# Level masks on VectorE two levels ahead, all row squares on GpSimd, four softplus parts among the third attention's last blocks

## The chip, the cores and the metric

The kernel runs on one core of one Trainium2 chip. Time is the device time of one execution in microseconds. Before the change it is 5413.46 us, the median of three runs (5405.54 to 5415.52).

## The reference, cut to what matters

Two decoder layers over x (64 x 128 x 256, float32) with a context of the same shape. Every residual block starts with a layer norm.

```
x += L0_attn(ln(x))    # gated delta rule, 2 heads of 128, chunks of 64
x += L0_xattn(ln(x))   # cross attention, 16 heads
x += L0_ffn(ln(x))     # 4 experts of width 512, top 2
x += L1_attn(ln(x))    # latent attention, causal
x += L1_xattn(ln(x))   # cross attention, causal
x += L1_ffn(ln(x))     # 8 experts of width 128, top 2
# in L0_attn, per chunk of 64 rows
log_decay = -exp(A_log) * softplus(x @ W_alpha.T + dt_bias)
cum = cumsum(log_decay);  L_mask = tril(exp(cum_i - cum_j))
M = tril(-(wk_scaled @ wk.T) * L_mask, -1)
A = inverse(eye - M)              # unit lower triangular
```

The first layer norm and the decays are computed with error-free sums and products (pairs of a value and its rounding rest), the rest in plain float32.

## The kernel before, in words

A loop of 16 passes takes four sequences each. Every engine has its own instruction list, written by hand and repeated with `Fori`; they meet only in semaphores, whose counts are written into the waits (`S[...]`, `sum_step`, `chain_step`, `au_ready`, `y_ready`). There is no planner: the order in the source is the order on each engine.

In one pass TensorE, ScalarE and VectorE carry the blocks in the order of the reference. The delta rule's inverse is built in six levels. `first_level` (L1635 on) makes MT, the level-0 matrix and `Um`. At level l, TensorE transposes `Um` (L1089) to `Tm`, multiplies it with a masked copy of MT, `lev[l % 2]` (L1067, counted in `W_psum`), multiplies the result with `Um` (L1074, `U_psum`), and VectorE adds that to `Um` (L1823). The read scores (L1046) and the values (L1054) go between levels on TensorE. The masked copies, MT times `levmask[l]`, are made by GpSimd at L647, two heads a level, twelve a pass.

GpSimd works ahead in the background on the decay projection of the next pass's rows. Its chain has four slices of 64 columns; each is 22 products (`chain_products`, 128x256 elements) and 16 links (`chain_links`, eight operations on 128x32). It is counted in `chain_step`. Slice 0's products lie between the level masks, in the shares of `LEVEL_PRODUCTS`. Between links GpSimd adds rows to the residual `xres`, after waits for the layer norm (`xn`), the root of the exact norm (`ref_step`), the mixture's statistics (`hl_mean`) and the router's gates (`g_w`); `ROUTER_LINKS` and the numbers in the calls say how many links lie between these. The chain ends with `au` (L678). Then `centered` sums and centres the rows of the pass after next (L503, the last step is a 128x1024 subtraction in `x_in`), and GpSimd waits for `y_ready`, makes the squares and adds rows 0 to 15 of 32 (`first_squares`), and builds the decay table (`decay_table`, which ends with `dec_beta`, needed by `first_level`). SP moves `x_in` to `xn_next` once `chain_step` has reached `CHAIN_READ`, and then loads the next x.

VectorE adds the other sixteen rows (`exact_squares(16, 32)`, L1425) in four pieces during the level stage, behind a wait for `sum_step`, and then takes the variance.

Softplus of `au` is a list of ten parts of three or four small operations on 128x10 elements (`decay_exponential`, tile `dec_t`), each behind a wait for its predecessor, followed by a quotient, a series, and `y_nat` (L1596). In the third attention VectorE runs 16 score blocks u (L1854 takes the maximum, L1858 subtracts it, both read PSUM) and, for each b of four, two operations on the outputs (L1875, L1877) that TensorE waits for at L1199. Parts 0 to 4, with the wait for `au`, lie ahead of the output operations of b = 2, parts 5 to 7 ahead of b = 3; parts 8 and 9 come after the last xT copy, ahead of the gates.

Of the kernel before, what the change touches and what calls it, by code (L numbers as in the profile page):

```python
# [12 lines left out]
ALU = mybir.AluOpType  # L13
# [6 lines left out]
P = 128  # L20
D = 256
C = D // P
G = 4
# [6 lines left out]
DH = 2  # L30
# [41 lines left out]
def decoder_kernel(nc, a, out):  # L72
# [7 lines left out]
    with ExitStack() as ctx:  # L80
# [362 lines left out]
        def _(pool):  # L443
# [79 lines left out]
            def first_squares(it, a):  # L523

                tt = pool.tensor_tensor
                w8 = sq.rearrange("p b (k n) -> p b k n", n=32)
                sum_link(it, a, tt, sq, x_in[:, :, :], x_in[:, :, :], ALU.mult)
                sum_link(it, a, tt, lan2[:, :, :], w8[:, :, :, 0], w8[:, :, :, 1], ALU.add)
                for k in range(2, 16):
                    sum_link(it, a, tt, lan2[:, :, :], lan2[:, :, :], w8[:, :, :, k], ALU.add)  # L530
                assert summed[0] == SUM_STEPS, summed[0]

# [92 lines left out]
            decay_table(0, 0)  # L625

            with nc.Fori(0, NIT, engines=[pool.engine], hint_back_edge=True) as it:
# [12 lines left out]
                for l in range(1, LEVELS):  # L640
                    chain_products(pool, link, src, 0, LEVEL_PRODUCTS[l - 1], LEVEL_PRODUCTS[l])
                    for h in range(DH):
                        if l == 1 and h == 0:
                            pool.wait_ge(S["inv_eye"], at(it, "inv_eye", 2))
                        if l > 2:
                            pool.wait_ge(S["W_psum"], at(it, "W_psum", 2 * (l - 3) + h + 1))
                        pool.tensor_tensor(heads(lev[:, l % 2, h, :]), heads(MT[:, h, :]),  # L647
                                           levmask[:, l, :].unsqueeze(1).broadcast_to([P, G, P]), ALU.mult).then_inc(S["lev"], 1)

# [4 lines left out]
                chain_links(pool, link, 0, 0, 5)  # L654
# [3 lines left out]
                chain_links(pool, link, 0, 5, 16)  # L658
# [12 lines left out]
                chain_links(pool, link, 3, 0, 8)  # L671
                pool.wait_ge(x_norm, nth(it, 1, 1, 2))
                assert linked[0] < CHAIN_READ, linked[0]
                chain_links(pool, link, 3, 8, 16)
# [7 lines left out]
                decay_table(it, 1)  # L682

# [682 lines left out]
        def _(dve):  # L1366
# [365 lines left out]
            with nc.Fori(0, NIT, engines=[dve.engine], hint_back_edge=True) as it:  # L1732
# [76 lines left out]
                xT_copy(0)  # L1809
                wait("ctx_psum", 2)  # L1810
                dve.tensor_copy(ctxT[:, 1, :], bank[3][:, :]).then_inc(S["ctxT_dve"], 1)
                dve.wait_ge(sum_step, nth(it, SUM_STEPS, SUM_STEPS))
                exact_squares(16, 21)
# [6 lines left out]
                for l in range(1, LEVELS - 1):  # L1820
                    for h in range(DH):
                        wait("U_psum", 2 * (l - 1) + h + 1)
                        dve.tensor_tensor(Um[:, h, :], Um[:, h, :], bank[4 + h][:, :], ALU.add).then_inc(S["U"], 1)  # L1823
                    if l == 1:
                        read_decays(0)
                        exact_squares(21, 25)
                    if l == 2:
                        read_decays(1)
                        exact_squares(25, 29)
                    if l == 3:  # L1830
                        exact_squares(29, 32)
                        exact_variance()
# [15 lines left out]
                def attention(a_no):  # L1848
                    base = a_no * QUADS
                    for u in range(QUADS + 8):  # L1850
                        if u < QUADS:
# [7 lines left out]
                            if a_no == 1 and u % 2:  # L1859
                                exact_rest(1, u // 4, u // 2 % 2)  # L1860
                        if u >= 6 and (u - 6) % 4 == 3 and (u - 6) // 4 < G:
# [5 lines left out]
                            if a_no == 2 and b == 2:  # L1867
                                for part in range(5):
                                    decay_exponential(part)
                            if a_no == 2 and b == 3:  # L1870
                                for part in range(5, 8):
# [193 lines left out]
                decay_exponential(8)  # L2065
# [33 lines left out]
ROUTER_LINKS = 5  # L2099
REF_STEPS = 75  # L2100
CHAIN_READ = 530
PRODUCTS = 22
LEVEL_PRODUCTS = (0, 4, 4, 8, 14, 19, 22)
ROOT_STEPS = 41
# [3 lines left out]
SUM_STEPS = 37  # L2108
# [30 lines left out]
```

## Time and profile before

| | |
|---|---|
| median of three runs | 5413.46 us |
| the profiled execution | 5405.82 us |
| its span, first to last instruction | 5403.9 us |
| TensorE busy | 4731.9 us (88%) |
| VectorE busy | 4303.5 us (80%) |
| GpSimd busy | 3938.4 us (73%) |
| ScalarE busy | 2323.7 us (43%) |
| mean granted TensorE clock | 0.954 |

The profile is of one execution. A line such as L1823 is a line of the kernel, PE is TensorE, DVE VectorE, ACT ScalarE, POOL GpSimd. PE has two sets of rows, its matmuls and its weight loads (PEld). Times in a timeline count from the first instruction. Most SBUF tiles are cuts of one tensor, `arena`, so many rows name only that.

### The profile page before, as it was taken

Reading aid. Unit: us, or ns where it says so; the run is one execution under the profiler, and the core shown is the slowest. Engines: PE = TensorE matmul, PEld = TensorE weight load, DVE = VectorE, ACT = ScalarE, POOL = GpSimd, SP = SyncE. Lnnn points to the kernel's source line nnn. Section 1 sums busy time; section 2 is a strip of 40 time slices with the busy share of each in tenths; the row PEclk is TensorE's granted clock in tenths of the full one; section 3 lists DMA queues with packets and bytes.
Section 4 is the critical chain, followed back from the end, with each engine's and each line's share of the span. In section 5 each row is a group of like instructions: output and inputs, shape, how many; then the busy total and the mean of one; then the engine's idle time right before and its main releaser. Section 6 shows DMA issues by size and latency. Waiting matters only on the chain.

```text
span 5403.9 us, 105986 instructions
## 1 busy us (share of the span) xinstructions
PE 4731.9 (88%) x28362; PEld 3086.5 (57%) x28362; DVE 4303.5 (80%) x11377; ACT 2323.7 (43%) x4480; POOL 3938.4 (73%) x10789
## 2 busy tenths in 40 slices
PE   1089999999999999999999999998999999899999
PEld 0065656656565565656556565664656556565655
DVE  8878788787878877787877778777787887878788
ACT  0044444454444444443444544445444444444444
POOL 7478686777868678686767868676785867778686
PEclk7599999999999999999999999999999999999999
DMA  3000000000000000000000000000000000000000
GB/s 89 8 13 9 21 1 25 5 9 21 1 29 1 25 5 9 21 1 29 1 13 17 9 21 1 25 5 9 21 9 21 1 25 5 9 21 1 21 1 17
DMA packets 61894, 78.20 MB, mean 14 GB/s; under 512 B 11168, under 2 KB 53808, under 8 KB 61232
## 3 DMA queue, kind: packets, MB, share of 16 engines
q1 hardware_dynamic: 52784, 62.42, 3.6%
q10 hardware_dynamic: 8448, 8.39, 0.4%
q8 instruction: 240, 3.93, 0.3%
q14 instruction: 422, 3.46, 0.2%
HBM read 45.04 MB, written 8.46 MB: 10 GB/s over the span
## 4 chain that ended last, share of the span: by engine, by line
PE 33%; POOL 29%; DVE 21%; issue 11%; ACT 4%; POOLq 2%; DMA 0%; DVEq 0%; ACTq 0%; SPq 0%
POOL acc_c L635 11%; POOL arena L635 6%; PE bank L1331 3%; PE bank L1238 3%; POOL acc_a L635 3%; POOL acc_b L635 3%; POOL acc_s L635 3%; POOL sl_t L635 2%; PE bank L1191 2%; DVE arena L2088 2%; PE bank L1067 2%; POOLq L634 2%; PE bank L1074 2%; PE bank L1157 2%; PE bank L1143 2%
## 5 line engine op out<-in xcount | busy, mean ns | idle before, releaser
L1854 DVE TENSOR_REDUCE smax<-bank 128x4 f32<-128x512 f32 x768 | 525.2, 684 | 92.3 <-PE bank L1149 51.0
L817 ACT ACTIVATE arena<-bank 128x512 f32<-128x512 f32 x768 | 454.9, 592 | 249.4 <-PE bank L1157 243.7
L1858 DVE TENSOR_TENSOR arena<-bank,smax 128x512 f32<-128x512 f32 x768 | 531.2, 692 | 26.4
L1157 PE MATMUL bank<-ident,arena 128*128 128x128 f32 x3072 | 485.8, 281 | 43.0 <-ACT arena L804 25.7
L1238 PE MATMUL bank<-w,arena 128*128 128x512 f32 x1024 | 490.4, 610 | 14.0 <-DVE arena L1806 14.0
L1143 PE MATMUL bank<-arena 64*128 64x512 f32 x1536 | 440.2, 650 | 64.4 <-ACT arena L841 28.0
L1157 PEld LDWEIGHTS bank<-ident,arena 128*128 128x128 f32 x3072 | 346.9, 141 | 242.9 <-ACT arena L806 82.2
L1271 PE MATMUL bank<-w,arena 128*128 128x256 f32 x2048 | 454.1, 380 | 13.9 <-ACT arena L876 13.9
L804 ACT ACTIVATE arena<-arena,rstd 128x512 f32<-128x512 f32 x512 | 368.1, 719 | 197.9 <-DVE arena L1858 193.4
L1271 PEld LDWEIGHTS bank<-w,arena 128*128 128x128 f32 x2048 | 387.8, 190 | 90.3 <-issue 23.0
L635 POOL TENSOR_TENSOR acc_a<-acc_s,arena 128x32 f32<-128x32 f32 x1008 | 262.1, 260 | 175.4 <-DVE gate L1973 51.8
L876 ACT ACTIVATE arena<-bank,lnb,lng 128x512 f32<-128x512 f32 x256 | 197.3, 777 | 442.1 <-PE bank L1256 439.3
L1169 PE MATMUL bank<-arena 128*32 128x128 f32 x6144 | 327.5, 285 | 57.1 <-ACT arena L810 54.5
L949 PE MATMUL bank<-causal,identb 128*128 128x512 bf16 x658 | 158.5, 380 | 201.9 <-DVE y_nat L1596 198.9
L635 POOL TENSOR_TENSOR acc_c<-acc_a,acc_b 128x32 f32<-128x32 f32 x1008 | 265.7, 264 | 79.7
L635 POOL TENSOR_TENSOR acc_s<-acc_a,acc_c 128x32 f32<-128x32 f32 x1008 | 266.0, 264 | 78.9
L635 POOL TENSOR_TENSOR acc_c<-acc_c,arena 128x32 f32<-128x32 f32 x1008 | 264.4, 262 | 78.8
L635 POOL TENSOR_TENSOR acc_b<-acc_a,acc_s 128x32 f32<-128x32 f32 x1008 | 264.0, 262 | 78.8
L635 POOL TENSOR_TENSOR acc_c<-acc_c,acc_d 128x32 f32<-128x32 f32 x1008 | 262.5, 260 | 78.9
L503 POOL TENSOR_TENSOR arena<-arena 128x1024 f32<-128x1024 f32 x17 | 32.2, 1893 | 394.2 <-DVE y_nat L1596 394.1
L635 POOL TENSOR_TENSOR arena<-arena,sl_t 128x256 f32<-128x256 f32 x384 | 289.2, 753 | 27.6
L647 POOL TENSOR_TENSOR arena<-arena,levmask 128x512 f32<-128x512 f32 x192 | 239.8, 1275 | 65.6 <-DVE arena L1643 65.6
(437 smaller groups left out, 11962.0 us busy)
## 6 DMA issues: line engine op xcount, KB each, us to landing
arena<-in_x_dram SPq DMA_DIRECT2D x35, 512.0 KB, 3.6
xn_next<-arena SPq DMA_DIRECT2D x17, 512.0 KB, 2.9
arena<-cum_dram SPq DMA_DIRECT2D x17, 512.0 KB, 3.8
arena<-in_ctx_dram SPq DMA_DIRECT2D x16, 512.0 KB, 3.7
out_dram<-arena ACTq DMA_DIRECT2D x16, 512.0 KB, 3.1
xn<-xn_next SPq DMA_DIRECT2D x15, 512.0 KB, 3.0
w<-in_L_ffn_w_dram SPq DMA_DIRECT2D x8, 512.0 KB
w<-in_L_ffn_w_dram SPq DMA_DIRECT2D x1, 1024.0 KB
```

Source lines behind the costliest of these rows:

```text
L635: operation(*operands).then_inc(chain_step, 1)
L647: pool.tensor_tensor(heads(lev[:, l % 2, h, :]), heads(MT[:, h, :]), levmask[:, l, :].unsqueeze(1).broadcast_to([P, G, P]), ALU.mult).then ...
L804: act.activation(Ssb[:, v % 4], Ssb[:, v % 4], ACT.Exp, scale=rstd[:, v // 4:v // 4 + 1]).then_inc(S["p_exp"], 1)
L817: act.activation(PT[:, v % 2], bank[3 + v % 2][:, :].rearrange("p (h q) -> p h q", h=QH), ACT.Copy).then_inc(S["pt"], 1)
L876: act.activation(zT[:, e % 2, k, :], bank[4 + n % 2][:, :], ACT.Relu, scale=lng[:, e, k:k + 1], bias=lnb[:, e, k:k + 1]).then_inc(S["zT"], 1)
L1143: ins = mm(bank[S_BANKS[v % 4]][:, :], QT[rows, c, g * P:(g + 1) * P], KM[rows, g, min(c, chunks - 1)].rearrange("p h t -> p (h t)"), star ...
L1157: ins = tr(bank[3 + v % 2][:, j * P:(j + 1) * P], Ssb[:, v % 4, j, :], ident[:, :])
L1169: ins = mm(bank[5][2 * HD * j:2 * HD * (j + 1), (v % 4) * P:(v % 4 + 1) * P], V2[:, g, (v % 4) * QH + j, :], PT[:, v % 2, j, :], start=Tru ...
L1238: ins = mm(bank[g][:, :], xT[:, c, g * P:(g + 1) * P], w1_0[:, e, c, :], start=(c == 0), stop=(c == C - 1))
L1271: ins = mm(bank[6 + g // 2][:, (g % 2) * D:(g % 2 + 1) * D], zT[:, e % 2, k, g * P:(g + 1) * P], w2_0[:, e, k, :], start=(k == 0), stop=(k ...
L1854: dve.tensor_reduce(smax[:, u, :], sc, AX, ALU.max).then_inc(S["s_max"], 1)
L1858: dve.tensor_tensor(Ssb[:, u % 4], sc, smax[:, u, :].unsqueeze(2).broadcast_to([P, QH, P]), ALU.subtract).then_inc(S["s_sub"], 1)
```

## The change

VectorE makes the level masks: (1,0) and (1,1) around the context copy, both of level 2 ahead of the level loop, and after the additions of level l those of level l + 2. The xT copy of the first layer norm moves behind mask (1,1). VectorE's sixteen row additions go, and GpSimd makes them (`second_squares`) after the decay table; the wait for `sum_step` now stands ahead of the variance. GpSimd has no masks; slice 0's products stand in one piece, and the numbers of links between its waits change: 5 then 4 before the `xn` wait in place of 5, 9 of slice 1 before the gate wait in place of 5, 10 of slice 3 before the `x_norm` wait in place of 8. Softplus parts 0 to 3 move behind score blocks 12 to 15 of the third attention, parts 4 and 5 stand ahead of b = 2, parts 6 to 8 ahead of b = 3, and part 9 remains after the xT copy.

```diff
+            def second_squares(it, a):
+                w8 = sq.rearrange("p b (k n) -> p b k n", n=32)
+                for k in range(16, 32):
+                    sum_link(it, a, pool.tensor_tensor, lan2[:, :, :], lan2[:, :, :], w8[:, :, :, k], ALU.add)
...
-                for l in range(1, LEVELS):
-                    chain_products(pool, link, src, 0, LEVEL_PRODUCTS[l - 1], LEVEL_PRODUCTS[l])
-                    for h in range(DH):
-                        if l == 1 and h == 0:
-                            pool.wait_ge(S["inv_eye"], at(it, "inv_eye", 2))
-                        if l > 2:
-                            pool.wait_ge(S["W_psum"], at(it, "W_psum", 2 * (l - 3) + h + 1))
-                        pool.tensor_tensor(heads(lev[:, l % 2, h, :]), heads(MT[:, h, :]),
-                                           levmask[:, l, :]...).then_inc(S["lev"], 1)
+                chain_products(pool, link, src, 0)
+                chain_links(pool, link, 0, 0, INPUT_LINKS)
...
-                chain_links(pool, link, 0, 0, 5)
+                chain_links(pool, link, 0, INPUT_LINKS, NORM_LINKS)
                 pool.wait_ge(S["xn"], at(it, "xn", 4))
...
-                chain_links(pool, link, 0, 5, 16)
+                chain_links(pool, link, 0, NORM_LINKS, 16)
...
-                chain_links(pool, link, 3, 0, 8)
+                chain_links(pool, link, 3, 0, 10)
                 pool.wait_ge(x_norm, nth(it, 1, 1, 2))
-                chain_links(pool, link, 3, 8, 16)
+                chain_links(pool, link, 3, 10, 16)
...
                 first_squares(it, 1)
                 decay_table(it, 1)
+                second_squares(it, 1)
...
-                xT_copy(0)
+                def level_mask(l, h):
+                    if l > 2:
+                        wait("W_psum", 2 * (l - 3) + h + 1)
+                    dve.tensor_tensor(heads(lev[:, l % 2, h, :]), heads(MT[:, h, :]),
+                                      levmask[:, l, :]..., ALU.mult).then_inc(S["lev"], 1)
+                level_mask(1, 0)
                 wait("ctx_psum", 2)
                 dve.tensor_copy(ctxT[:, 1, :], bank[3][:, :]).then_inc(S["ctxT_dve"], 1)
-                dve.wait_ge(sum_step, nth(it, SUM_STEPS, SUM_STEPS))
-                exact_squares(16, 21)
+                level_mask(1, 1)
+                xT_copy(0)
+                for h in range(DH):
+                    level_mask(2, h)
...
+                    if l + 2 < LEVELS:
+                        for h in range(DH):
+                            level_mask(l + 2, h)
                     if l == 1:
                         read_decays(0)
-                        exact_squares(21, 25)
                     if l == 2:
                         read_decays(1)
-                        exact_squares(25, 29)
                     if l == 3:
-                        exact_squares(29, 32)
+                        dve.wait_ge(sum_step, nth(it, SUM_STEPS, SUM_STEPS))
                         exact_variance()
...
+                            if a_no == 2 and 12 <= u:
+                                decay_exponential(u - 12)
...
                             if a_no == 2 and b == 2:
-                                for part in range(5):
-                                    decay_exponential(part)
+                                decay_exponential(4)
+                                decay_exponential(5)
                             if a_no == 2 and b == 3:
-                                for part in range(5, 8):
+                                for part in range(6, 9):
                                     decay_exponential(part)
...
                 xT_copy(5)
-                decay_exponential(8)
                 decay_exponential(9)
...
-ROUTER_LINKS = 5
-REF_STEPS = 75
-CHAIN_READ = 530
+ROUTER_LINKS = 9
+INPUT_LINKS = 5
+NORM_LINKS = 9
+REF_STEPS = 59
+CHAIN_READ = 546
-LEVEL_PRODUCTS = (0, 4, 4, 8, 14, 19, 22)
-ROOT_STEPS = 41
+ROOT_STEPS = 25
-SUM_STEPS = 37
+SUM_STEPS = 53
```

## Rows read from the trace of the kernel before

**Rows 1.** The page: busy time by engine, and the last chain's shares.
```profile
PE 4731.9 (88%) x28362; PEld 3086.5 (57%) x28362; DVE 4303.5 (80%) x11377; ACT 2323.7 (43%) x4480; POOL 3938.4 (73%) x10789
...
PE 33%; POOL 29%; DVE 21%; issue 11%; ACT 4%; POOLq 2%; DMA 0%; DVEq 0%; ACTq 0%; SPq 0%
```

**Rows 2.** Waits over the span: who waited for whom: us, times, longest.
```profile
POOL arena L503 <- DVE y_nat L1596: 394.1, 16, 26.7
...
POOL arena L647 <- DVE arena L1643: 65.6, 15, 5.5
...
PE bank L1199 <- DVE arena L1877: 28.7, 26, 2.8
...
DVE dec_t L1511 <- POOL au L678: 16.7, 13, 2.3
...
PE bank L1089 <- DVE arena L1823: 8.2, 16, 0.6
```

**Rows 3.** Timeline, first level: start, us, engine, line, operation, [idle before].
```profile
2840.93 0.69 DVE L1641 TENSOR_TENSOR arena<-arena,levmask 128x512 f32<-128x512 f32 x1
...
2846.19 4.70 DVE L1425 TENSOR_TENSOR lan<-lan,arena 128x32 f32<-128x32 f32 x5
...
2850.18 1.06 PE L1046 MATMUL bank<-rkT 128*128 128x128 f32 x8
...
2851.02 1.29 DVE L1823 TENSOR_TENSOR arena<-arena,bank 128x512 f32<-128x512 f32 x2
...
2851.76 1.26 PE L1089 MATMUL bank<-ident,arena 128*128 128x128 f32 x8 [0.52 <-DVE arena L1823]
```

**Rows 4.** Timeline of VectorE and TensorE in the expert stage.
```profile
2969.24 0.69 DVE L1398 TENSOR_TENSOR arena<-arena 128x512 f32<-128x512 f32 x1
...
2979.46 2.97 DVE L1998 TENSOR_SCALAR arena<-bank,umv,urs 128x512 f32<-128x512 f32 x4
...
2982.48 0.66 PE L1256 MATMUL bank<-ident,arena 128*128 128x128 f32 x4
...
2993.45 0.62 DVE L1764 TENSOR_TENSOR uparts<-uparts 128x4 f32<-128x4 f32 x1
...
3003.10 1.10 DVE L1398 TENSOR_TENSOR arena<-arena 128x512 f32<-128x512 f32 x1
...
3005.93 0.88 DVE L2010 SCALAR_TENSOR_TENSOR arena<-bank,gate,arena 128x256 f32<-128x256 f32 x2 [0.19 <-DVE arena L1468]
```

**Rows 5.** GpSimd's row additions, two ends of links; line L1474 (ns min/median/max).
```profile
2822.37 4.74 POOL L503 TENSOR_TENSOR lan<-lan,arena 128x32 f32<-128x32 f32 x14
...
2877.63 0.25 POOL L635 TENSOR_TENSOR acc_s<-acc_a,acc_c 128x32 f32<-128x32 f32 x1
...
2880.02 0.25 POOL L635 TENSOR_TENSOR acc_s<-acc_a,acc_c 128x32 f32<-128x32 f32 x1
...
L1474 DVE SCALAR_TENSOR_TENSOR arena<-arena,row x272: 474/485/978, 35.1 to 5294.5; 128x256 f32<-128x256 f32 x136
```

**Rows 6.** Timeline of the third attention's tail, VectorE and TensorE.
```profile
2787.01 0.27 DVE L1511 TENSOR_TENSOR dec_t<-au,a_row 128x8 f32<-128x8 f32 x1 [0.86 <-POOL au L678]
...
2790.82 0.26 DVE L1875 RECIPROCAL orec<-bank 128x16 f32<-128x16 f32 x1
...
2791.59 0.44 PE L1199 MATMUL bank<-ident,arena 128*128 128x128 f32 x2 [1.34 <-DVE arena L1877]
```

**Rows 7.** Timelines: GpSimd's 128x1024 operations and VectorE steps that met them.
```profile
4070.68 1.89 POOL L503 TENSOR_TENSOR arena<-arena,row 128x1024 f32<-128x1024 f32 x1
...
4070.72 1.88 DVE L1536 TENSOR_SCALAR dec_t<-dec_t 128x10 f32<-128x10 f32 x1
...
2954.30 2.22 DVE L1927 TENSOR_TENSOR arena<-arena,lt_mask 128x16 f32<-128x16 f32 x1
```

**Rows 8.** Another pass: TensorE's idle, and windows around both tails (PEclk ninth value).
```profile
3109.99 0.44 PE L1199 MATMUL bank<-ident,arena 128*128 128x128 f32 x2 [2.81 <-DVE arena L1877]
...
2787.00:2797.00 10.00, 8.15 (x70) 5.78 (x71) 7.97 (x38) 4.41 (x10) 7.88 (x21) 1.00 0.02 4
3110.00:3117.00 7.00, 7.00 (x34) 5.12 (x35) 4.16 (x19) 1.74 (x5) 4.14 (x10) 0.76 0.00 1
```

More of the change, by code:

```diff
@@ L625, in _ @@
             decay_table(0, 0)
+            second_squares(0, 0)
             with nc.Fori(0, NIT, engines=[pool.engine], hint_back_edge=True) as it:
@@ L639, in _ @@
                 pool.wait_ge(moved_next, nth(it, 16, 16))
-                for l in range(1, LEVELS):
-                    chain_products(pool, link, src, 0, LEVEL_PRODUCTS[l - 1], LEVEL_PRODUCTS[l])
-                    for h in range(DH):
-                        if l == 1 and h == 0:
-                            pool.wait_ge(S["inv_eye"], at(it, "inv_eye", 2))
-                        if l > 2:
-                            pool.wait_ge(S["W_psum"], at(it, "W_psum", 2 * (l - 3) + h + 1))
-                        pool.tensor_tensor(heads(lev[:, l % 2, h, :]), heads(MT[:, h, :]),
-                                           levmask[:, l, :].unsqueeze(1).broadcast_to([P, G, P]), ALU.mult).then_inc(S["lev"], 1)
+                chain_products(pool, link, src, 0)
+                chain_links(pool, link, 0, 0, INPUT_LINKS)
                 pool.wait_ge(loaded_r, nth(it, 16, 16))
@@ L1806, in xT_copy @@
                     dve.tensor_copy(xT[:, 1, :], bank[XT_BANKS[s][1]][:, :]).then_inc(S["xT_dve"], 1)
-                xT_copy(0)
+                def level_mask(l, h):
+                    if l > 2:
+                        wait("W_psum", 2 * (l - 3) + h + 1)
+                    dve.tensor_tensor(heads(lev[:, l % 2, h, :]), heads(MT[:, h, :]),
+                                      levmask[:, l, :].unsqueeze(1).broadcast_to([P, G, P]), ALU.mult).then_inc(S["lev"], 1)
+                level_mask(1, 0)
                 wait("ctx_psum", 2)
                 dve.tensor_copy(ctxT[:, 1, :], bank[3][:, :]).then_inc(S["ctxT_dve"], 1)
-                dve.wait_ge(sum_step, nth(it, SUM_STEPS, SUM_STEPS))
-                exact_squares(16, 21)
+                level_mask(1, 1)
+                xT_copy(0)
+                for h in range(DH):
+                    level_mask(2, h)
                 def read_decays(h):
```

## The prediction

> **What bounds the kernel now.** I read the shares of busy time and of the last chain first, then the list of waits, then one loop pass in order of time. TensorE is busy 88% of the span, VectorE 80%, GpSimd 73%; the chain that ended last lies 33% on TensorE, 29% on GpSimd, 21% on VectorE [rows 1]. GpSimd's share there is no bound on a pass: it idles 394 us for `y_nat`, near 25 us in each of 16 passes, and 65.6 us for the last `Um` before its first mask. What others wait for from GpSimd is one thing, `au`: 16.7 us, 13 times [rows 2]. So work taken off GpSimd pays only where it brings `au` forward or changes what VectorE runs beside. A pass takes 320 us, so one microsecond a pass is 16 us, 0.3% of the whole. All else is read from single stretches.
>
> **The level stage.** VectorE loses sixteen row additions and gets twelve masks. Beside GpSimd's masks the additions are slow (five took 4.70 us) and make VectorE late: they end at 2850.89, L1823 starts at 2851.02, and TensorE sits 0.52 us before its transposes, its read scores (L1046) having ended at 2851.24 [rows 3]; in all 8.2 us in 16 times [rows 2]. A mask has the form of L1641 (128x512, two SBUF inputs), 0.69 us with GpSimd idle [rows 3]; L1398, the same form, took 0.69 beside GpSimd's small links and 1.10 beside its 128x256 products [rows 4]. The new order from 2844.4, when the last `Um` is there: mask (1,0) to 2845.5, context copy 2845.6 to 2846.3 (it waits for TensorE as before), mask (1,1) to 2847.4, xT copy to 2848.1, masks (2,0) and (2,1) to 2849.5 at 0.69 or 2850.3 at 1.10. The addition has to start by 2850.6 if TensorE is to go on straight from its read scores. So it is in time and the 0.52 us go. No more goes: after that TensorE's matmuls and ScalarE's copies set the 5.5 to 6.9 us of a level, and VectorE's two additions (1.3), two masks (1.4 to 2.2) and one read (0.7) fit. The masks' waits, for W matmuls two levels back, are met. Against it: W of head 1 needs mask (1,1) just when it comes; and the sixteen additions given to GpSimd (14 took 4.74 us [rows 5], so 5.4) fill its idle time ahead of the masks and end near 2843.8, the products behind them. If a product starts before the last L1643 (2843.70), that takes 1.10 in place of 0.69 and all levels are 0.4 late. Between 0.52 gained and 0.1 lost I take 0.45 gained, nearer to the clean order.
>
> **GpSimd.** Off come 12 masks of 1.27 us and the wait of 4.4 us before them; on come 5.4 us of additions. That does not reach the end of the pass: 22 products (0.8 each), 5 links, the residual addition and 4 more links end near 2884, while the layer norm that it then waits for is ready only near 2893. What passes on are those four links: one is eight operations, 2.39 us [rows 5], so 9.6 us. They are repaid before the gate wait (9 links of slice 1 in place of 5), and behind the gate GpSimd is 9.6 us ahead for good. I take 1 us off for links that will run beside VectorE's large quotient operations: `au` comes 8.7 us earlier (8 to 10). The move of x and the load behind it on SP's queue shift forward alike and start 16 us ahead of `au`, enough for two transfers of 3 to 4 us each.
>
> **The expert stage: two collisions trade places.** The slice-2 products now run from 2989.5 to 3008.1, beside VectorE's L1622 to L1468, and the accumulation L2010 follows at 3005.93 though its matmuls were done near 3005.5 [rows 4]. The products move to about 2979 to 2997; those operations then lie beside links: 0.4 gained. But at 2979 VectorE makes the root of expert 2 in small steps; one such step (L1764) took 0.62 us beside products in expert 3. The z behind it ends at 2982.43, and TensorE starts on it at 2982.48, without slack [rows 4]: 0.4 lost. Sum 0, ends -0.4 and +0.45.
>
> **Second attention.** Slice-3 products cover two more of the eight L1474, which take 0.485 us in the median and 0.978 at most [rows 5]. Between 0 and 0.8 lost; I take 0.2, as most are near the median.
>
> **Third attention's tail: the main term.** Now VectorE is through with the scores at 2786.15, waits 0.86 for `au`, makes 17 small steps of 0.205 us and reaches the reciprocal at 2790.82; TensorE sits 1.34 us before L1199 [rows 6], 28.7 us in all such waits [rows 2]. New: parts 0 to 3 (13 steps) behind blocks 12 to 15, parts 4 and 5 (8 steps) ahead of the reciprocal. From 2779.49: 1.33 for block 12, 0.92 for part 0, 1.33 and 0.62, 0.7 for the two o operations of b = 1, 1.33 and 0.62, 1.33 and 0.62, 8 x 0.205: 2790.1, 0.7 earlier; with the mean wait for `au` (16.7/16 = 1.04) in place of 0.86 it is 0.9. `au`, then at 2778.3, is in time for part 0 at 2780.8.
> But GpSimd's centering comes forward with `au`. Its last step, the 128x1024 subtraction, starts 7.9 us behind `au` and takes 1.89. Where it met a small VectorE step, that took 1.88 us in place of 0.17, and a 128x1024 addition stretched L1927 to 2.22 [rows 7]. In this pass it fell on operations that read PSUM. Now it will run from about 2786.0 to 2787.9, and VectorE's steps stand at 2785.8 to 2786.4 and from 2787.8 on. The page "GPSIMD Engine Reference" of the Trainium skill (8. Key points) says that GpSimd contends with VectorE instructions that have two SBUF inputs or a 2-port mode; by that rule score blocks, which read PSUM, are free and the moved parts are not, so it speaks against just this move, and the rows agree. Cost 0.5 to 1.85, by phase; I take 1.3. Tail: -0.9 + 1.3 = +0.4 a pass, ends -0.9 and +1.0. The o operations of b = 1 come 1.7 later; TensorE's L1199 there shifts by 0.3, hidden as long as the later one waits for VectorE.
>
> **Behind it.** Part 8 goes (3 steps, 0.6) from between xT copy and gates, but the router logits end on TensorE only 0.3 before VectorE now asks for them, and TensorE hardly ever waits for `y_nat`. 0 to 0.2 gained; I take 0.1. The first pass's level stage loses its wait on GpSimd's row sums: 1 us once.
>
> **Sum.** -0.45 + 0 + 0.2 + 0.4 - 0.1 = +0.05 a pass, 1 us in 16, less 1 once: 0. The profiled execution took 5405.8 us (span 5403.9), 7.6 below the median of the three timed runs, 5413.5. A change of 0 on that median: 5413 us.
>
> **Rivals.**
> (A) Faster: the subtraction misses the small steps. Between two groups of them lie 1.4 us of PSUM-only work, and in this pass it misses them; against it, it is 1.89 us long and the steps are now spread over the whole window. Then -0.45 - 0.4 (expert 2 spared too) + 0.1 - 0.9 - 0.1 = -1.75 a pass, 28 us: 5385. Half of this, some passes hit and some not, gives 5399 and is as likely.
> (B) Slower, by the clock: the granted clock stayed at 1.00 behind an idle of 1.34 us, but was 0.76 over 7 us behind one of 2.81 [rows 8]. If the subtraction costs its full 1.85, TensorE's idle goes from 1.5 to 2.4 us in most passes: +0.9. Seven us at 0.76 lose 1.7 us of matmul time; in the half of the passes that are clean today that is another +0.9 a pass. With the level gain +1.35 a pass, 22 us: 5435. It decides from an idle of about 2 us on. "TensorE: Matmul & The Clock Gate" of the Trainium skill (Part 1) has the clock follow how busy the engine has lately been; by that, too, a longer idle brings this about.
> (C) It does not do what it says: mask (1,1) comes too late for W and the 0.52 us stay. +0.5 a pass: 5421.
>
> **How the numbers follow.** What this measurement can tell from no change is about 0.2%, 11 us. Forecast 0.28 and C 0.08 lie within it: 0.36. A and its half: 0.34. B 0.18, and the bad ends of tail, expert and second attention together (+1.0 + 0.45 + 0.8 - 0.5 = +1.75, 5441) 0.12: 0.30. The likeliest case's own range is 5402 to 5424; the range of 8 in 10 reaches from A to B: 5384 to 5438.
>
> **What would show it.** L1089 behind the first level without its 0.52 us; masks on VectorE at 0.69 to 1.10; no wait for `au`; the 1.89 us subtraction beside steps on dec_t, one of them over 1 us; idle before L1199 near 1.9 us in the third attention. I am wrong if that idle is under 1 us in most passes (A), or if the addition of level 1 still starts straight behind VectorE's queue.

## The result, and the profile after

The changed kernel takes 5367.35 us (median of 4, 5356.80 to 5372.72) against 5414.49 us (median of 4) of the kernel before: ratio 0.9913, 95% interval 0.9898 to 0.9928, some 2.9 us less in each of 16 passes. I had forecast 5413 us. In three later measurements the same kernel came out at 0.9883, 0.9946 and 0.9963 (intervals of some 0.0015 to either side), so it is faster each time, but by 20 to 63 us; why it moves so is part of what the experiments settle.

The page after, beside [rows 1]: GpSimd has left the last chain.
```profile
PE 4669.8 (87%) x28362; PEld 3054.6 (57%) x28362; DVE 4166.0 (78%) x11313; ACT 2320.8 (43%) x4480; POOL 3868.1 (72%) x10869
...
PE 59%; DVE 27%; issue 8%; ACT 5%; POOL 0%; DVEq 0%; DMA 0%; ACTq 0%; SPq 0%; POOLq 0%
```
The waits after, beside [rows 2]: `L1511 <- au` and `L1089 <- addition` are gone, GpSimd idles 6.6 us more a pass before `y_nat`, TensorE's waits at L1199 are hardly less in sum (26.3 against 28.7) but none is over 1.7 us.
```profile
POOL arena L503 <- DVE y_nat L1596: 499.2, 16, 33.2
...
PE bank L1089 <- DVE arena L1643: 26.4, 30, 1.9
PE bank L1199 <- DVE arena L1889: 26.3, 34, 1.7
```
I cut each pass at four events and took means over the 16 passes of both profiles:

| from, to | before | after | change | predicted |
|---|---|---|---|---|
| gates to reciprocal of b = 2 in the third attention | 150.23 | 148.27 | -1.96 | +0.6 (0 + 0.2 + 0.4) |
| that reciprocal to `y_nat` | 29.78 | 28.32 | -1.46 | -0.1 |
| `y_nat` to the second `Um` of `first_level` | 24.44 | 25.23 | +0.79 | 0 |
| `Um` to gates | 115.39 | 114.97 | -0.42 | -0.45 |

The sum is -3.05 us a pass, 48.8 us, and the two profiled executions differ by 49.0. The first row is where the prediction failed, the second in part, the fourth is right. Taken apart, the first row is: gates to the last xT copy of the experts -0.12, from there to the second attention's first block -2.01, from there to block 12 of the third attention 0.00, from that block to the reciprocal +0.18.

**The first row.** Timeline of before in pass 9 (start, us, engine, line, operation, [idle before and what ended it]): gates, `au`, reciprocal.
```profile
2959.08 0.17 DVE L1973 TENSOR_TENSOR gate<-gtop,grc 128x16 f32<-128x16 f32 x1
...
3105.18 0.20 POOL L678 TENSOR_TENSOR au<-acc_a 128x8 f32<-128x8 f32 x1
...
3109.22 0.26 DVE L1875 RECIPROCAL orec<-bank 128x16 f32<-128x16 f32 x1
```
`au` stands 146.10 us behind the gates, the reciprocal 4.04 behind `au`. In 14 of 16 passes the second number is 4.03 to 4.44, and the first is 145.7 to 146.3 in all: in the kernel before, this stretch ends with GpSimd's chain, whatever TensorE does in it (experiment 2 tests this). After the change, pass 9:
```profile
2930.10 0.18 DVE L1985 TENSOR_TENSOR gate<-gtop,grc 128x16 f32<-128x16 f32 x1
...
3066.24 0.20 POOL L677 TENSOR_TENSOR au<-acc_a 128x8 f32<-128x8 f32 x1
...
3078.27 0.26 DVE L1887 RECIPROCAL orec<-bank 128x16 f32<-128x16 f32 x1 [0.37 <-DVE dec_t L1530]
```
`au` stands 136.14 behind the gates, 9.8 us earlier on the mean (8.7 forecast) and 12 us ahead of the reciprocal. No row shows VectorE waiting for it any more.

**TensorE's clock at the end of the experts.** Timeline of TensorE in pass 9, before, and a window around it (the value behind the busy times of the five engines is the granted clock, 1.00 for 2.4 GHz and 0.50 for 1.2):
```profile
3016.04 0.66 PE L1020 MATMUL bank<-ident,arena 128*128 128x128 f32 x4 [0.86 <-DVE arena L1984]
3017.78 3.33 PE L1281 MATMUL bank<-arena,Wcd 128*128 128x512 f32 x4 [1.08 <-DVE arena L1806]
```
```profile
3014.00:3024.00 10.00, 7.37 (x25) 3.29 (x24) 6.53 (x26) 2.17 (x6) 8.08 (x32) 0.83 0.01 2
```
and after:
```profile
2988.06 0.66 PE L1020 MATMUL bank<-ident,arena 128*128 128x128 f32 x4 [0.57 <-DVE arena L1996]
2989.80 1.95 PE L1281 MATMUL bank<-arena,Wcd 128*128 128x512 f32 x4 [1.08 <-DVE arena L1806]
```
```profile
2986.00:2996.00 10.00, 7.42 (x31) 3.66 (x29) 7.77 (x29) 2.38 (x7) 8.16 (x32) 1.00 0.00 1
```
Before, the clock is at half behind this place in all 16 passes, and the four L1281 take 3.33 us in place of 1.95. After, in none. TensorE's idle before L1020 is 0.73 to 1.02 us before and 0.53 to 0.57 after. From the last xT copy of the experts to the second attention's first block it was 12.01 us and is 10.00, and this is all of the first row.

The idle grew shorter because VectorE no longer comes late to the last expert's outputs: in pass 9 it starts on them 3.25 us ahead of TensorE's next work (L974) in place of 3.01, and is done with them that much sooner. Timeline of VectorE, before:
```profile
3004.24 1.50 DVE L1468 TENSOR_SCALAR arena<-arena,row 128x256 f32<-128x256 f32 x2
3005.93 0.88 DVE L2010 SCALAR_TENSOR_TENSOR arena<-bank,gate,arena 128x256 f32<-128x256 f32 x2 [0.19 <-DVE arena L1468]
```
and after, with GpSimd's products gone from beside it:
```profile
2974.41 0.69 DVE L1468 TENSOR_SCALAR arena<-arena,row 128x256 f32<-128x256 f32 x2
2978.01 0.88 DVE L2022 SCALAR_TENSOR_TENSOR arena<-bank,gate,arena 128x256 f32<-128x256 f32 x2 [2.91 <-PE bank L1271]
```

**The level stage** did what was forecast. VectorE and TensorE in the first level of pass 9, and GpSimd ahead of it:
```profile
2815.95 1.21 DVE L1813 TENSOR_TENSOR arena<-arena,levmask 128x512 f32<-128x512 f32 x1
...
2817.82 1.16 DVE L1813 TENSOR_TENSOR arena<-arena,levmask 128x512 f32<-128x512 f32 x1
...
2822.14 0.69 DVE L1832 TENSOR_TENSOR arena<-arena,bank 128x512 f32<-128x512 f32 x1 [0.23 <-PE bank L1074]
...
2822.84 1.04 PE L1089 MATMUL bank<-ident,arena 128*128 128x128 f32 x8
...
2806.56 5.44 POOL L503 TENSOR_TENSOR lan<-lan,arena 128x32 f32<-128x32 f32 x16
```
The sixteen additions take 5.44 us (5.4 forecast), the second addition waits for TensorE again, and L1089 starts without the 0.52 us of [rows 3]. Here they end late, at 2812.0, so the products meet `first_level` and the masks (1.2 us each; over all 192 masks the median is 0.83). The level stage gave -0.42 in sum; the way into it, the third row of the table, lost more than that.

**The tail of the third attention**, pass 10:
```profile
3391.34 1.89 POOL L503 TENSOR_TENSOR arena<-arena,row 128x1024 f32<-128x1024 f32 x1
...
3392.86 0.40 DVE L1524 TENSOR_TENSOR dec_t<-dec_t 128x10 f32<-128x10 f32 x1
...
3396.45 0.44 PE L1199 MATMUL bank<-ident,arena 128*128 128x128 f32 x2 [0.91 <-DVE arena L1889]
```
The subtraction lies mostly beside score blocks, which read PSUM and keep their 0.69 us; the small step behind it, L1524, takes 0.40 to 0.47 in seven passes, this one among them, and 1.17 to 1.26 in eight; in one pass another step takes 1.86. Block 12 to the reciprocal is 11.66 us against 11.48, then TensorE waits 0.91 or 1.7 us (1.46 in the first pass). Before it waited 1.3 to 2.8 in most passes, and in half of them a half-clock stretch followed [rows 8]; after there is none, and reciprocal to reciprocal takes 3.17 us in every pass against 3.86 on the mean.

### The profile page after: what moved, and what is told of

Its sections match the earlier page's. It is cut to its first block, busy times and chain, and to the rows that moved or that the text cites. A ratio compares the mean times of both kernels' runs of the same rounds, so it can differ in the third digit from the quotient of the medians.

```text
span 5355.1 us, 105890 instructions
## 1 busy us (share of the span) xinstructions
PE 4669.8 (87%) x28362; PEld 3054.6 (57%) x28362; DVE 4166.0 (78%) x11313; ACT 2320.8 (43%) x4480; POOL 3868.1 (72%) x10869
## 3 DMA queue, kind: packets, MB, share of 16 engines
q14 instruction: 407, 3.33, 0.2%
## 4 chain that ended last, share of the span: by engine, by line
PE 59%; DVE 27%; issue 8%; ACT 5%; POOL 0%; DVEq 0%; DMA 0%; ACTq 0%; SPq 0%; POOLq 0%
PE bank L1238 5%; PE bank L1331 4%; PE bank L1357 4%; PE bank L1271 4%; PE bank L1143 4%; PE bank L1157 4%; DVE smax L1864 4%; PE bank L1191 3%; PE bank L1067 3%; PE bank L1169 3%; PE bank L1074 3%; DVE arena L1474 2%; DVE arena L2010 2%; PE bank L1256 2%; PE bank L1149 1%
## 5 line engine op out<-in xcount | busy, mean ns | idle before, releaser
L1271 PEld LDWEIGHTS bank<-w,arena 128*128 128x128 f32 x2048 | 387.8, 190 | 90.3 <-issue 23.0
L642 POOL TENSOR_TENSOR arena<-arena,sl_t 128x256 f32<-128x256 f32 x384 | 306.2, 797 | 30.1
L1238 PEld LDWEIGHTS bank<-w,arena 128*128 128x128 f32 x1024 | 182.0, 194 | 166.7 <-issue 149.4
```

Source lines behind the costliest of these rows:

```text
L642: operation(*operands).then_inc(chain_step, 1)
L1238: ins = mm(bank[g][:, :], xT[:, c, g * P:(g + 1) * P], w1_0[:, e, c, :], start=(c == 0), stop=(c == C - 1))
L1271: ins = mm(bank[6 + g // 2][:, (g % 2) * D:(g % 2 + 1) * D], zT[:, e % 2, k, g * P:(g + 1) * P], w2_0[:, e, k, :], start=(k == 0), stop=(k ...
```

## The experiments

All are full kernels timed in five rounds beside the kernel before on the same chip. Stage times are means over the 16 passes of the run's profile.

### 1. Two filling matmuls more or fewer at the end of the experts

```
-MIX_FILL = 14
+MIX_FILL = 16        # on the kernel before; 12 on the changed kernel
```


> The kernel before with two more bf16 filling matmuls between the two halves of the fourth block's transposes (MIX_FILL 16 for 14; they are 0.227 us each, so TensorE's idle before L1020 at the end of the experts falls from 0.86 to 1.02 us to 0.4 to 0.6 us, the 0.56 us of the changed kernel). Nothing else differs. Theory 1 (clock: the half-clock stretches that began 0.5 to 4 us behind that idle in every pass go away when the idle is short): the stretch from the last xT copy of the experts to the first score block of the second attention falls from 12.0 to about 10.0 us in every pass, so about 32 us less in all: 5382 us, ratio 0.994. Theory 2 (contention: the 2.0 us came from GpSimd's products no longer lying beside VectorE there): no change, 5414 us, and the half-clock stretches stay.

Measured: 1.0016 (1.0007 to 1.0025), slower. The idle before L1020 fell to 0.46 us on the mean, the half-clock stretches there went in 14 of 16 passes, and the stage fell from 12.01 to 10.19 us, as the clock theory has it. But VectorE's wait for `au` grew from [rows 2]'s 16.7 us to
```profile
DVE dec_t L1511 <- POOL au L678: 37.4, 16, 2.7
```
and gates to reciprocal hardly moved, from 150.23 to 149.80 us. The longer idle in the tail was followed by half-clock stretches there in 15 passes. So of the 1.8 us that the half clock took at the end of the experts, the kernel before could get back only 0.4 by the reciprocal: `au` hid the rest. Both my theories for this run were incomplete.

> The changed kernel with two filling matmuls fewer at the same place (MIX_FILL 12): idle before L1020 goes from 0.56 to about 1.02 us. Theory 1 (clock): the half-clock stretches come back at this place in most passes, the stretch to the second attention goes from 10.0 to about 12.0 us, about +32 us: 5399 us, ratio to before 0.997. Theory 2 (contention): no change, 5367 us, ratio 0.9913.

Measured: 0.9944 (0.9931 to 0.9956), 16 us above the changed kernel's first result. The time alone shows little, for the changed kernel itself came to 0.9946 once (section 6); the profile does. Idle 1.03 us, stretches in 15 of 16 passes, the stage 12.67 us in place of 10.00, gates to reciprocal 151.51 in place of 148.27. With `au` out of the way the clock is paid for, and with the clock at half the earlier `au` brings nothing: 151.51 is more than the 150.23 of the kernel before.

### 2. GpSimd's `au` earlier and later, in the kernel before

```
-ROUTER_LINKS = 5
+ROUTER_LINKS = 6     # and 4 in a second kernel
```


> The kernel before with one link more ahead of GpSimd's wait for the gates (ROUTER_LINKS 6 for 5); nothing else. GpSimd idles 3.2 us there in each pass, one link takes 2.39 us, so au comes about 2.4 us earlier. Theory 3 (from the two runs just made: in the kernel before the time from the gates to the third attention's reciprocal of b = 2 is 149.9 us in 13 of 16 passes, whatever TensorE's clock did in between, because it is au plus 4.04 us; GpSimd sets it): that time falls to what TensorE and VectorE need, 148.8 to 149.5 with this filling, 0.4 to 1.1 us a pass, 6 to 18 us: 5396 us, ratio 0.998. Rival (the wait for au is worth only itself, 1.04 us, and the collision of the 128x1024 subtraction with the small steps takes most of it back): 0 to -5 us.

Measured: 0.9905 (0.9890 to 0.9920), 50 us less by one number. Pass 9:
```profile
2932.06 0.18 DVE L1973 TENSOR_TENSOR gate<-gtop,grc 128x16 f32<-128x16 f32 x1
...
2989.63 0.66 PE L1020 MATMUL bank<-ident,arena 128*128 128x128 f32 x4 [0.56 <-DVE arena L1984]
...
3075.64 0.20 POOL L678 TENSOR_TENSOR au<-acc_a 128x8 f32<-128x8 f32 x1
...
3079.68 0.26 DVE L1875 RECIPROCAL orec<-bank 128x16 f32<-128x16 f32 x1
```
`au` comes 143.58 us behind the gates and the reciprocal again 4.04 behind it: GpSimd still sets this stretch, 147.6 us long in most passes. And the slice-2 products, now 2.4 us earlier, no longer lie beside L1468 (0.35 us each against 0.70 and 0.88), so the idle before L1020 is 0.56 us and the half-clock stretches are gone there in 13 of 16 passes. In two of the other three TensorE sets the end: 153.12 and 152.51 us, with the reciprocal 10 us behind `au`. I had expected only 18 us, since I had not seen that link.

> The kernel before with one link fewer ahead of GpSimd's wait for the gates (ROUTER_LINKS 4 for 5): au comes 2.39 us later behind the gates. Theory (GpSimd's au sets the time from the gates to the third attention's reciprocal): that time goes from 149.9 to 152.3 us in every pass, +2.4 us a pass, 38 us, ratio 1.007 (1.005 to 1.011: longer TensorE idle in the tail can bring more half-clock time). Rival (au costs only the wait that VectorE shows for it, 1.04 us a pass on the mean, with slack in the passes that wait least): +1 to +1.5 us a pass, ratio 1.003 to 1.004.

Measured: 1.0100 (1.0086 to 1.0115). Gates to reciprocal 152.82 us, 2.6 more; the wait for `au` is now
```profile
DVE dec_t L1511 <- POOL au L678: 84.0, 16, 5.8
```
and the reciprocal follows `au` by 4.03 us in all passes. The rest, 1.4 us from the reciprocal to `y_nat` and 0.9 behind it, goes with half-clock stretches of 6.8 us in every tail. GpSimd's `au` as the bound of this stretch in the kernel before is shown from both sides.

> The same with MIX_FILL 16 as well, so that TensorE's idle at the end of the experts is short and the half-clock stretches there go. Alone this filling brought 1.83 us a pass at that place and lost 1.31 of it in the wait for au. Theory 3 (GpSimd's au held back what the clock gave): with au 2.4 us earlier the gain arrives: gates to reciprocal 147.5 to 148.3, -1.7 to -2.4 us a pass, 27 to 38 us: 5380 us, ratio 0.994. Rival (the half-clock stretches only move to another place, whatever au does): no better than the kernel with one link alone, 5400 us or more.

Measured: 0.9883 (0.9868 to 0.9898). Idle before L1020 0.15 us, no stretch, gates to reciprocal 147.33. The two numbers alone give 64 us, as much as the whole change gave on that chip (0.9883, after_again).

### 3. Parts of the change

```
 # masks_alone: the changed kernel with
-ROUTER_LINKS = 9, NORM_LINKS = 9, links 10 of slice 3, CHAIN_READ = 546
+ROUTER_LINKS = 5, NORM_LINKS = 5, links 8 of slice 3, CHAIN_READ = 530
 # and, as in a_soft_old:
-if a_no == 2 and 12 <= u: decay_exponential(u - 12)
-b == 2: parts 4, 5;    b == 3: parts 6 to 8;  behind xT_copy(5): 9
+b == 2: parts 0 to 4;  b == 3: parts 5 to 7;  behind xT_copy(5): 8, 9
```


> Masks on VectorE and all squares on GpSimd, but the numbers of links between GpSimd's waits as before (5, 5 of slice 1, 8 of slice 3), and the softplus parts in their old places. au is then not earlier, the tail of the third attention as before (idle 1.04 us for au, half-clock stretches in half of the passes). Level stage -0.44 us a pass = -7 us. Theory 1 (the half-clock stretch at the end of the experts hangs on TensorE's idle before L1020, which is decided by what GpSimd runs beside the mixture norm and so by where the slice-2 products lie): between 5375 and 5407 us, according to whether the idle there is near 0.56 or 0.9 us; the profile must show both or neither. Rival (the masks themselves bring all of the gain): 5367 us, with the tail's half-clock stretches gone too.

Measured: 0.9943 (0.9930 to 0.9956), 26 us less. The profile has -0.91 us a pass (of it -0.32 in the level stage, -0.40 from the tail's reciprocal to `add_y`, -0.28 at the end of the experts) and 0.9 once at the start, 15 us; `au` stays 145.8 behind the gates and the reciprocal 3.86 behind it; the idle before L1020 is 0.87, with half-clock stretches in 14 passes. So my rival, that the masks and squares alone bring all of the gain, falls: the half-clock stretches at the end of the experts and the wait in the tail are still there. Of the 26 us the profiles show 15: the profiled execution, the slowest of five, is 6 us over their median, and the profile of the kernel before is 5 us under the median that it had beside this run. No row explains these 11 us.

> The changed kernel with the softplus parts back in their old places (0 to 4 ahead of b = 2, 5 to 7 ahead of b = 3, 8 behind the xT copy), masks, squares and link numbers as changed. Part 8 behind the xT copy: +0.6 us a pass, 10 us. In the third attention the wait for au stays away (it is 9.8 us earlier), VectorE reaches the reciprocal at 5.25 + 1.3 + 17 x 0.205 = 10.1 us behind block 12 plus a collision with the 128x1024 subtraction (7.6 us behind block 12, in the middle of the small steps, up to 1.7): 11.0 to 11.8 against 11.66 now, so 0 to -0.6 us a pass. Theory 1 (earlier au pays through the softplus parts' new places only for part 8): about +5 us, 5372 us. Rival (the spread parts are what keeps TensorE's idle in short pieces and the clock up in the tail): the half-clock stretches behind block 12 come back in half of the passes, +0.9 + 0.6 a pass: +20 us or more, 5390 us.

Measured: 0.9931 (0.9918 to 0.9944), 5374 us, near the 5372 expected; but the changed kernel was not timed beside it and differs by more than that from one measurement to the next, so only the stages tell. Part 8 back on the path costs 0.72 us a pass. Block 12 to the reciprocal takes 10.08 us in nine passes, as expected, and up to 11.82 in others. Behind that reciprocal the next is over 4 us away in 4 passes, so the rival has a part. In this profile, its slowest execution (5406 us), half-clock stretches are back at the end of the experts with an idle of 0.58 to 0.62 us, in 14 passes; that place has nothing to do with the edit.

### 4. The collision with the 128x1024 subtraction

```
 def centered(it, a):
     ...
-    sum_link(..., x_in[:, :, :], x_in[:, :, :], row[:, 0, :]..., ALU.subtract)
 ...
     pool.wait_ge(y_ready, nth(it, 1, 2))
+    sum_link(..., x_in[:, :, :], x_in[:, :, :], row[:, 0, :]..., ALU.subtract)
     first_squares(it, 1)
```


> The changed kernel with GpSimd's 128x1024 subtraction moved behind its wait for y_nat, away from the softplus steps of the third attention. It now meets VectorE only around y_nat, where VectorE waits for TensorE. Theory (the collision costs the tail 0.2 us in half of the passes and 1.0 in the other half, read from the 0.40 to 1.26 us steps at L1524): from block 12 to the reciprocal of b = 2 falls from 11.1 to 12.0 us to about 10.9, -0.3 to -0.7 us a pass, 5 to 11 us, ratio 0.2% below the changed kernel's of this call. As predicted blind (the collision costs 1.3 us a pass): 21 us, 0.4% below it. Rival (TensorE's own work sets the end there, or squares and decay table come 1.9 us later and delay the level stage): no gain.

Measured: 0.9988 (0.9980 to 0.9997), slower than the changed kernel beside it (0.9946) by 0.4%. Block 12 to the reciprocal fell from 11.66 to 10.90 us: 0.76 us a pass is what the collision had cost. But the 128x1024 squares behind it moved onto `cum_all`. GpSimd, then VectorE, pass 9:
```profile
2813.81 1.89 POOL L503 TENSOR_TENSOR arena<-arena,row 128x1024 f32<-128x1024 f32 x1 [32.79 <-DVE y_nat L1601]
2815.78 1.90 POOL L503 TENSOR_TENSOR arena<-arena 128x1024 f32<-128x1024 f32 x1
...
2815.95 1.87 DVE L1610 TENSOR_TENSOR cum_all<-cum_all,run_pre 8x128 f32<-8x128 f32 x1
```
In the changed kernel the same addition misses them:
```profile
2791.51 0.28 DVE L1605 TENSOR_TENSOR cum_all<-cum_all,run_pre 8x128 f32<-8x128 f32 x1
```
TensorE waits for `cum_all`, so `y_nat` to the first output sum grew by 1.9 us, and the way from there to the first level's additions, with GpSimd's row sums now later, by another 1.5. The rival that I had named (squares and decay table late) is at most the weaker half of what happened; the stronger, this step, I had not named.

> The same with MIX_FILL 16. TensorE's idle before L1020 goes from 0.55 us (where executions of the changed kernels had no half-clock stretch at 0.53 to 0.57 us, some at 0.58 to 0.64) to about 0.1 us. Expected: no half-clock stretch there in any execution, a narrower spread of times (under 8 us), and a time at or up to 5 us below that of the kernel with the later subtraction alone. Rival (the filling delays L1020, or stretches move on): slower by 0.1 us a pass or more.

Measured: 0.9983 (0.9974 to 0.9992). No half-clock stretch at the end of the experts, idle 0.17 us, all 11 executions within 10 us, but no gain over the kernel above beyond their intervals: the 1.9 us behind `y_nat` stays.

### 5. More filling elsewhere

```
-keep_busy(8, 4)
+keep_busy(16, 4)      # behind the router logits
+if c == 0 and g == 2 and s == 5: keep_busy(3, 2)     # in to_features
 to_features(5)
+keep_busy(3, 2)
 xT_ready(5)
```


> The changed kernel with more filling matmuls where half-clock stretches are left: 16 for 8 behind the router logits (TensorE idles 2.19 us there), three between the second and third transposes of the last block and three ahead of its xT wait (0.79 and 0.88 us idle). Clock theory: the stretches near 130 and 300 us behind y_nat go, in the profile of the changed kernel 6 and 16 of them; each costs 1 to 2 us where TensorE sets the end: 16 to 30 us less, 5342 us, ratio 0.987. Rival (stretches move on to the next idle): 5367 us, ratio 0.991.

Measured: 0.9920 (0.9906 to 0.9933), 25 us slower than the changed kernel beside it, at a higher mean clock (0.971 in the middle of its executions against 0.967). The stretches near 130 and 300 us behind `y_nat` went, and others came at 5, 29 and 292 us, in the level stage and in the tail, where TensorE sets the end: the rival. But the profile is of one of its slowest executions (5411 us, clock 0.963), so it does not show where those at 0.971 lost their time.

### 6. Why the changed kernel moves between measurements

> The changed kernel as it is, to have its time on this chip beside the others and a second profile: 5367 us, ratio 0.9913. By the clock theory the time of its executions follows the mean granted clock, and the third attention's tail and the end of the experts stay free of half-clock stretches in most passes of this profile too.

Measured: 0.9883 (0.9868 to 0.9898); four executions within 5 us; no half-clock stretch at the end of the experts, idle 0.54 to 0.57 us.

> The changed kernel as it is, so that the others of this call have it on the same chip. Ratio between 0.988 and 0.992, as in its two earlier calls; the higher of these with half-clock stretches at the end of the experts in some executions, the lower without.

Measured: 0.9946 (0.9930 to 0.9962); executions from 5374 to 5405 us. Its profile has the stretches in 14 of 16 passes, with idles of 0.59 to 0.64 us. Gates to reciprocal takes 151.34 us on the mean of these 14 and 148.39 in the two without, with `au` at its early place in all. Pass 8, timeline of TensorE and a window:
```profile
2692.94 0.66 PE L1020 MATMUL bank<-ident,arena 128*128 128x128 f32 x4 [0.59 <-DVE arena L1996]
2694.68 3.08 PE L1281 MATMUL bank<-arena,Wcd 128*128 128x512 f32 x4 [1.08 <-DVE arena L1806]
```
```profile
2695.00:2713.00 18.00, 15.56 (x38) 6.30 (x36) 9.53 (x28) 5.57 (x13) 14.56 (x61) 0.53 0.00 1
```


> The changed kernel as it is, beside the others of this call: 0.988 to 0.995 of before. By the theory its ratio goes with the half-clock stretches at the end of the experts in its profile: none, then about 0.988; in most passes, then 0.991 to 0.995.

Measured: 0.9963 (0.9949 to 0.9978); executions from 5355 (the profiled one, idle 0.56, one stretch) to 5407 us.

```
-MIX_FILL = 14
+MIX_FILL = 16        # on the changed kernel
```


> The changed kernel with MIX_FILL 16: TensorE's idle before L1020 about 0.15 us. Theory (the changed kernel stands at an edge with its idle of 0.55 to 0.62 us, and on one chip or in one execution falls to one side of it, in another to the other): no half-clock stretch at that place, executions within 10 us of each other, ratio 0.987 to 0.989 whatever the unfilled kernel does on this chip. Rival (its differences between calls come from elsewhere): the same ratio and the same spread as after_fourth.

Measured, beside after_fourth: 0.9867 (0.9853 to 0.9881), four executions within 8 us. Pass 9:
```profile
2993.51 0.66 PE L1020 MATMUL bank<-ident,arena 128*128 128x128 f32 x4
2995.25 1.95 PE L1281 MATMUL bank<-arena,Wcd 128*128 128x512 f32 x4 [1.08 <-DVE arena L1806]
```
The idle is 0.13 us, no stretch. Two fillings take the changed kernel off the edge on which it stood, and it is then 51 us faster than without them on that chip.

### 7. What the runs point to

```
 # b_best: the kernel before with
-ROUTER_LINKS = 5, MIX_FILL = 14
+ROUTER_LINKS = 6, MIX_FILL = 16
-b == 3: parts 5 to 7;  behind xT_copy(5): 8, 9
+b == 3: parts 5 to 8;  behind xT_copy(5): 9
```


> The kernel before with ROUTER_LINKS 6, MIX_FILL 16 and softplus part 8 ahead of b = 3 in place of behind the xT copy: three small edits, no mask and no square moved. With the first two it took 0.9883 of the time before. Theory (part 8 stands on the path behind the xT copy, 0.72 us a pass between a changed kernel with and without it): xT copy to y_nat -0.6 us a pass, 9 us less: ratio 0.9866, 5338 us. Rival (gl_psum takes its place, or its three steps ahead of b = 3 delay that reciprocal as much): 0.9883.

Measured: 0.9864 (0.9849 to 0.9878), executions within 7 us, xT copy to `y_nat` -0.59 us a pass. This version, with no mask and no square moved, beats both kernels as they stand, and equals the changed kernel with the same filling (0.9867, measured on another chip).

> The changed kernel with MIX_FILL 16, softplus parts 0 to 4 together ahead of b = 2 and parts 5 to 8 together ahead of b = 3. From the profiles: with the parts together the reciprocal of b = 2 comes 0.96 us sooner behind block 12 than with four of them between the score blocks; part 8 stays off the path behind the xT copy; the idle at the end of the experts is filled. Against a_fill16 -0.5 to -0.9 us a pass, 8 to 15 us less: ratio 0.985 to 0.987, no worse than the three small edits alone (0.9864). Rival (the collision with the subtraction, up to 1.7 us on a small step in one block of 17 steps, takes it back): equal to a_fill16.

Measured: 0.9906 (0.9892 to 0.9920), 20 us worse than a_fill16 beside it: worse even than the rival, which had them equal. With the small steps together the subtraction falls on one in every pass. VectorE and GpSimd, pass 9:
```profile
3089.36 1.83 DVE L1513 TENSOR_SCALAR dec_t<-dec_t 128x8 f32<-128x8 f32 x1
...
3089.27 1.89 POOL L503 TENSOR_TENSOR arena<-arena,row 128x1024 f32<-128x1024 f32 x1
```
The reciprocal comes 11.64 to 11.72 us behind block 12 in 15 passes, above the 11.30 that a_fill16 has on the mean, and the one of b = 3 follows it 0.42 later. So here it pays to have four parts among the score blocks, which read PSUM. That this is so because they are sheltered there is argued from these rows, not tested: in a_soft_old the same steps together took 10.08 us where nothing met them.

## Why the prediction was wrong

**The step that failed** is "Sum 0" in the expert stage. I worked out that the slice-2 products would leave L1468 and L2010 (0.4 us) and stopped at VectorE: up to the last xT copy that gave -0.12. What I did not follow is that VectorE's lateness there is TensorE's idle before L1020, 0.91 us on the mean, and that the half clock behind it goes with that idle. It fell to 0.55 us, the half clock went in all 16 passes, and -2.01 us came between the last xT copy of the experts and the second attention, for which my sum had no term. That is the whole -1.96 of the first row. Where the changed kernel kept the half clock (after_third, 14 passes), gates to reciprocal grew by 0.74 us against the 0.6 forecast, and its 5391.6 us lie far nearer to the 5413. So how far off the forecast is depends on the execution.

Of the profiles read, the idle at 0.53 to 0.57 us was followed by half clock in 2 of 85 passes, at 0.58 to 0.64 in 38 of 52, from 0.73 on in 45 of 48. The Trainium skill, "TensorE: Matmul & The Clock Gate" (Part 1), has the clock follow how busy the engine has recently been; the filling runs agree in direction (0.91 to 0.46 us of idle, 16 stretches to 2).

**The price of `au`** was the second error, and it hid the first. I took the mean wait of VectorE, 1.04 us, as all that `au` could cost, and its share of 29% of the last chain as no bound. The wait showed only what VectorE had left over after TensorE's own losses in the same stretch. In the kernel before, gates to reciprocal was `au` plus 4.04 us in 13 of 16 passes and 4.44 in one. Runs with `au` 2.4 us later and earlier gave 152.8 and 148.1 in place of 150.2. So a gain at the end of the experts could not have arrived without the earlier `au` (b_fill16), and the earlier `au` alone brings nothing where the half clock stays (a_fill12: 151.51). The 1.96 us need both.

**The tail** itself was sized well: +0.18 from block 12 to the reciprocal against +0.4. Without the collision the new order gains 0.58 us (10.90 in a_sub_late against 11.48), not 0.9. (The steps that the prediction lists add up to 2789.9, not 2790.1, so by its own rows it would have been 1.1.)

**Rival B named the mechanism with the wrong sign.** It let the idle in the tail grow to 2.4 us and the clock fall, from an idle of about 2 us on. The idle is 0.91 or 1.7 us after, and the half-clock stretches of 8 passes went: -0.88 us from the reciprocal to the second of `add_y`. Nor does the length of one idle decide: behind 1.53 us before the clock fell in pass 5, behind 1.56 it did not in pass 3, behind 1.72 after it never did.

**The collision** is there at 0.76 us a pass (by taking it away), within 0.5 to 1.85, below the 1.3 taken: between A's two cases. It can touch a one-input step too: L1513 took 1.83 us in c_best. The page "GPSIMD Engine Reference" of the Trainium skill (8. Key points) has GpSimd contend with VectorE instructions that have two SBUF inputs or run in a 2-port mode. The trace agrees in that the score blocks kept 0.69 us and two-input steps on `dec_t` took up to 1.86; whether L1513 ran in such a mode no run here shows.

**Part 8** was priced at 0.1 and gave 0.59 (0.72 undone, 0.59 done alone): the router logits did not take its place. **Level stage** (-0.42 against -0.45) was right. In the **second attention** the score blocks ended 0.19 us later, as forecast (+0.2), but the third attention's first block came as before (49.61 us behind the second's against 49.62), so it cost nothing. **Behind `y_nat`** I had nothing, and +0.79 came: half-clock stretches 6 us behind it in nine passes against five, and products beside `first_level`, for which I had given the levels 0.4. With the level stage that makes +0.37 a pass for moving masks and squares in this profile, and -0.31 in that of masks_alone.

What stays open: 11 of the 26 us of masks_alone, and what shifts the idle from 0.56 to 0.60 us between executions of one program.

## What to carry to other kernels

A wait is the difference between two arrivals, not the worth of the later one: measure the stretch from the event that releases the slow engine to the one that needs its result, in every pass, and if it is constant while the stages within it vary, that engine sets it and gains elsewhere in it are given back. Before moving large work, shift one unit of it by one number in both directions. Where a short idle of TensorE stands near the point at which its clock falls, fill it with margin: the changed kernel, on that edge, differs by 50 us between executions, and is judged by where they happened to fall. Split the passes of one profile by whether the stretch is there: two passes without it beside fourteen with it showed here what it costs.

## What the runs showed of the hardware

A GpSimd operation of 128x1024 with SBUF inputs held up very small VectorE steps that began with it until it was done: 1.83 us for a one-input TENSOR_SCALAR of 128x8 (c_best) and 1.87 for an addition of 8x128 (a_sub_late; 0.28 alone). A 128x512 operation with one input in PSUM kept its 0.69 us beside it. Filling with bf16 matmuls raised the mean clock from 0.967 to 0.971 and made the kernel 25 us slower (a_fills); in the one execution profiled, half-clock stretches had moved to where TensorE sets the end.
